# A graph network kernel on one core: dense stage without GpSimd, sort stage with bias matmuls over all rows

## The reference, cut to what matters

```python
# L0, five times: message = h[src] * e * scale, summed by dst
h = leaky(x @ W1[l] + b1[l]) @ W2[l] + b2[l]
e = leaky(edge_attr_32 @ We1[l] + be1[l]) @ We2[l] + be2[l]
# L1: sum of neighbours, with degrees
rst = segment_sum((x * deg_out ** -0.5 @ weight)[src], dst) * deg_in ** -0.5 + bias
# L2, twice: attention over the edges, softmax over the edges of each dst, 2 heads
# L3: relu(x[src] + edge_attr_64), summed by dst
```

## Time and profile before

| what | us |
|---|---|
| median of 3 runs (8425.77 to 8462.65) | 8448.33 |
| the profiled execution, its own time | 8526.05 |
| its span, first to last instruction | 8524.4 |
| TensorE busy | 6618.3 (78%) |
| VectorE busy | 6072.1 (71%) |
| GpSimd busy | 3765.3 (44%) |
| ScalarE busy | 3076.6 (36%) |

### The profile page before, as it was taken

The page is one execution under the profiler, slowest core; times in us unless marked ns, Lnnn a source line. Parts: engine busy times, 40 slices in busy tenths (PEclk is TensorE's granted clock), DMA queues, the critical chain, the costliest instruction groups (busy, mean ns, idle before and its releaser), DMA issues. The chain is left out here.

```text
span 8524.4 us, 285239 instructions
## 1 busy us (share of the span) xinstructions
PE 6618.3 (78%) x79417; PEld 5068.7 (59%) x79424; DVE 6072.1 (71%) x17993; ACT 3076.6 (36%) x5080; POOL 3765.3 (44%) x5536
## 2 busy tenths in 40 slices
PE   5999999934444588788788787887777999999787
PEld 3555655623333467576566666665675777677676
DVE  7444444479999798789788798898554554455799
ACT  2443434412222444344343343343222333233344
POOL 2655666644443255355354454454994000000354
PEclk9888888865555798789798898888555999899999
DMA  3655555622222677577576576675232111111476
GB/s 85 168 163 158 164 163 164 168 54 56 57 57 56 193 174 176 129 176 175 131 175 165 139 175 151 154 175 145 104 116 84 67 64 44 60 69 63 109 191 168
DMA packets 1739057, 1083.39 MB, mean 127 GB/s; under 512 B 1256693, under 2 KB 1623980, under 8 KB 1729274
## 3 DMA queue, kind: packets, MB, share of 16 engines
q1 hardware_dynamic: 1105530, 739.41, 29.9%
q0 software_dynamic: 254336, 267.05, 13.7%
q10 hardware_dynamic: 379008, 74.48, 4.9%
HBM read 812.49 MB, written 266.72 MB: 127 GB/s over the span
## 5 line engine op out<-in xcount | busy, mean ns | idle before, releaser
L540 POOL DMA_DIRECT2D big<-rows x3384 | 1819.6, 538 | 3258.7 <-issue 2189.2
L1307 PE MATMUL ps<-big 128*128 128x64 bf16 x27072 | 1722.9, 204 | 528.8 <-DVE big L1753 312.8
L1307 PEld LDWEIGHTS ps<-big 128*128 128x128 bf16 x27072 | 1330.2, 102 | 890.4 <-issue 624.6
L810 POOL DMA_INDIRECT rows<-big x800 | 1007.6, 1260 | 754.3 <-ACT big L938 409.0
L1295 PE MATMUL ps<-big 128*128 128x64 bf16 x27072 | 1098.2, 202 | 102.2 <-DVE big L1768 41.3
L1295 PEld LDWEIGHTS ps<-big 128*128 128x128 fp8e4 x27072 | 988.6, 104 | 202.0 <-issue 145.5
L1034 ACT CAST big<-big 128x512 bf16<-128x512 f32 x940 | 581.2, 618 | 1153.5 <-DVE big L1781 1153.5
L1559 DVE SCALAR_TENSOR_TENSOR big<-big 128x1000 f32<-128x1000 f32 (+1 forms) x300 | 359.1, 1197 | 860.0 <-ACT big L923 603.5
L1040 ACT CAST big<-big 128x512 bf16<-128x512 f32 x1128 | 697.2, 618 | 586.6 <-issue 436.2
L1781 DVE TENSOR_TENSOR big<-ps,big 128x512 f32<-128x512 f32 x940 | 645.8, 687 | 275.2 <-PE ps L1295 261.8
L1256 PE MATMUL ps<-identb,big 128*128 128x128 bf16 x1504 | 341.4, 301 | 563.1 <-DVE big L1669 561.5
(11 more groups left out here) (259 smaller groups left out, 10337.1 us busy)
## 6 DMA issues: line engine op xcount, KB each, us to landing
big<-ohsD SPq DMA_DIRECT2D x564, 256.0 KB, 2.9
big<-ohdD SPq DMA_DIRECT2D x564, 256.0 KB, 3.5
big<-rows POOLq DMA_DIRECT2D x3384, 32.0 KB, 2.8
big<-rows SPq DMA_DIRECT2D x3384, 32.0 KB, 2.4
big<-maskD SPq DMA_DIRECT2D x50, 1600.0 KB, 6.6
big<-rows ACTq DMA_DIRECT2D x2256, 32.0 KB, 2.5
big<-keyT SPq DMA_DIRECT2D x100, 488.3 KB
maskD<-big SPq DMA_DIRECT2D x25, 1600.0 KB, 6.1
```

The costliest lines, as they stand in the source:

```text
L540: eng.dma_start(edge[:, s.r, j, :], rows[bass.ds(v[s.r * (hi - lo) + j - lo], P), col]).then_inc(landed[s.r], 16)
L810: pool.indirect_dma_start(out=rows[:, :], out_offset=bass.IndirectOffsetOnAxis(ap=sidx[0:EP, j, c:c + 1], axis=0), in_=stage[0:EP, j, c, : ...
L1307: last = pe.matmul(pacc[:, bass.ds(w[j], D)], hot[:, g.r, j * P:(j + 1) * P], parts[:, g.r, c, j * D:(j + 1) * D], start=False, stop=False ...
```

## The change

In the dense stage GpSimd has no work. `find_over` goes to ScalarE as a ReLU of c - 65534 (1 at saturation, 0 otherwise), and the product with `excess` goes into VectorE's addition. ScalarE takes the logarithm of 2 c + tiny instead of c + tiny, and the mask is min(1e28 * log, log) in one VectorE instruction: the logarithm of a count of 0 is negative and becomes about -4e29, those of counts above 0 are positive and stay. `far` and its semaphore are gone. ScalarE copies the even groups of each block and VectorE the odd ones (before: by the running number). In the sort stage the bias matmul takes all 128 rows, with zeros in `be2p` below the third, and the matmuls of zeros are 12 ahead of m = 0 in chunks with j = 0 alone and 1 ahead of each other bias matmul.

```diff
 GpSimd
-            def find_over(w, c):
-                pool.wait_ge(craw_loaded[w % RAW], 16 * (w // RAW + 1))
-                if w >= 2:
-                    pool.wait_ge(cfull_made, (w - 2) * CUTS + c + 1)
-                span = slice(c * CW, (c + 1) * CW)
-                pool.tensor_scalar(over_full[w % 2][:, span], craw[w % RAW][:, span], FULL, excess[:, 0:1], ALU.is_ge, ALU.mult).then_inc(over_made, 1)
-
-            def make_far(w, c):
...
-                pool.tensor_scalar(far[w % 2][:, span], cfull[w % 2][:, span], -1.0, -FAR, ALU.add, ALU.mult).then_inc(far_made, 1)
...
 ScalarE
+            def find_over(w, c):
+                act.wait_ge(craw_loaded[w % RAW], 16 * (w // RAW + 1))
+                if w >= 2:
+                    act.wait_ge(cfull_made, (w - 2) * CUTS + c + 1)
+                span = slice(c * CW, (c + 1) * CW)
+                act.activation(over_full[w % 2][:, span], craw[w % RAW][:, span], ACT.Relu, bias=step2[:, 2:3]).then_inc(over_made, 1)
...
-                act.activation(lnc[w % 2][:, span], cfull[w % 2][:, span], ACT.Ln, bias=tiny[:, 0:1]).then_inc(ln_made, 1)
+                act.activation(lnc[w % 2][:, span], cfull[w % 2][:, span], ACT.Ln, scale=2.0, bias=tiny[:, 0:1]).then_inc(ln_made, 1)
...
-                if tau % 2:
+                if k % 2 == 0:
...
+            for k in range(2 * CUTS):
+                find_over(k // CUTS, k % CUTS)
             for w in range(W):
                 for k in range(TURNS):
                     keep_counts(w, k)
                     if k < CUTS:
                         log_counts(w, k)
+                    elif w + 2 < W:
+                        find_over(w + 2, k - CUTS)
+                if w + 2 < W:
+                    for c in range(TURNS - CUTS, CUTS):
+                        find_over(w + 2, c)
 TensorE, sort
-                    for _ in range(12 if m == 0 else 0):
-                        pe.matmul(bank(4), zerob[:, :], each(iota1b[:, :], 4), start=True, stop=True)
-                    pe.matmul(to, onesb[0:3, 0:EP], be2p[0:3, p, :], start=True, stop=False, skip_group_check=True)
+                    for _ in range(12 if m == j == 0 else 1):
+                        pe.matmul(bank(4 + h), zerob[:, :], each(iota1b[:, :], 4), start=True, stop=True)
+                    pe.matmul(to, onesb[:, 0:EP], be2p[:, p, :], start=True, stop=False, skip_group_check=True)
 VectorE
+            dve.memset(step2[:, 2:3], 1.0 - FULL)
+            bc(dve.memset(be2p[:, :, :], 0.0))
...
-                    dve.wait_ge(far_made, (w - 1) * CUTS)
-                dve.tensor_tensor(cfull[w % 2][:, span], over_full[w % 2][:, span], craw[w % RAW][:, span], ALU.add).then_inc(cfull_made, 1)
+                dve.scalar_tensor_tensor(cfull[w % 2][:, span], over_full[w % 2][:, span], excess[:, 0:1], craw[w % RAW][:, span], ALU.mult, ALU.add).then_inc(cfull_made, 1)
...
-                if tau % 2 == 0:
+                if k % 2:
...
-                dve.wait_ge(far_made, w * CUTS + c + 1)
-                dve.tensor_tensor(lnc[w % 2][:, span], lnc[w % 2][:, span], far[w % 2][:, span], ALU.min).then_inc(mask_done, 1)
+                dve.scalar_tensor_tensor(lnc[w % 2][:, span], lnc[w % 2][:, span], STEEP, lnc[w % 2][:, span], ALU.mult, ALU.min).then_inc(mask_done, 1)
```

More of the change, by code:

```diff
@@ L48 @@
 FULL = 65535.0
+STEEP = 1e28
 JB = 4
@@ L135, in graph_kernel @@
         rowb = sb("rowb", [P, 3, D])
-        step2 = sb("step2", [P, 2])
+        step2 = sb("step2", [P, 3])
         tiny = sb("tiny", [P, 1])
@@ L287, in graph_kernel @@
         lnc = [carve(NP) for _ in range(2)]
-        far = [carve(NP) for _ in range(2)]
         ct = carve(CTS, 512)
@@ L408, in graph_kernel @@
         ln_made = sem("ln_made")
-        far_made = sem("far_made")
         mask_done = sem("mask_done")
@@ L1369, in _, with kept @@
                 last.then_inc(n_down, 1)
+            EVEN, ODD = (TURNS + 1) // 2, TURNS // 2
+            def kept(tau):
+                w, k = tau // TURNS, tau % TURNS
+                if k % 2:
+                    pe.wait_ge(ct_kept_v, w * ODD + k // 2 + 1)
+                else:
+                    pe.wait_ge(ct_kept_a, w * EVEN + k // 2 + 1)
             def turn_counts(w, k):
@@ L1375, in turn_counts @@
                 if tau >= 4:
-                    pe.wait_ge((ct_kept_v, ct_kept_a)[tau % 2], tau // 2 - 1)
+                    kept(tau - 4)
                 for a, v in enumerate(range(4 * k, min(4 * k + 4, W))):
@@ L1382, in sum_rows @@
                 tau = w * TURNS + k
-                pe.wait_ge((ct_kept_v, ct_kept_a)[tau % 2], tau // 2 + 1)
+                kept(tau)
                 if k == 0 and w >= 2:
```

## The result

The changed kernel takes 8220.69 us (median of 4 runs, 8166.69 to 8294.69) beside 8440.91 us (4 runs, 8425.77 to 8462.65) for the kernel before: a ratio of 0.9716, with a 95% interval of 0.9662 to 0.977. The run of 8294.69 us counts as slow and is left out of the ratio, which compares the means of the others (8202.69 and 8442.56 us), but not out of the median. By the medians it is faster by 220 us; forecast were 7946 us and a range from 7830 to 8150. The profiled execution took 8223.66 us, with a span of 8221.4.

What follows compares the result with a forecast made beforehand. It took TensorE and its clock to bound the sort stage and GpSimd the dense stage. Savings of 300 us in the sort and 202 us in the dense stage, off the 8448 us median, gave 7946 us, range 7830 to 8150.

Steps and rivals of the forecast that it cites:

- (e) to (j): Dense stage: GpSimd's 20.6 us a block go, its work moving to ScalarE and VectorE; a saving of 202 us.
- (i): Dense stage, order of work: raw counts loaded late by SP could hold ScalarE's copies and TensorE, 0 to 1 us.
- (j): Dense stage: block of 12.5 us, between VectorE's bound and a cold TensorE's, with the clock between 0.6 and 0.9.
- dense stage cold: Rival: TensorE stays at 1.2 GHz in the dense stage, 15.9 us a block, saving 117 us there, 8031 us; chance 0.18.
- ScalarE reloads tables: Rival: two table loads of 1.28 us a block in the dense stage, 11.9 us for ScalarE, some 7970 us; chance 0.03.
- (a): Sort stage, matmuls of zeros: 4.25 fewer a chunk on average, 0.93 us less, hiding nothing but a PSUM copy.
- (b): Sort stage, bias matmul over all rows instead of three: 0.96 us less a chunk, bounds 0 and 1.2.
- (c): Sort stage at 2.4 GHz: TensorE 11.6 us a chunk, GpSimd the floor at 12.4, giving TensorE 0.8 us of slack.
- (d): Sort stage, clock: a fall costs about 3.5 us without the zeros; 0.9 us a chunk after slack, result 13.3 us.
- Sort keeps its falls: Rival: full rows in the bias don't stop the sort's clock falls, 15.0 us a chunk, 8116 us; chance 0.12.
- the pair of both rivals: Dense stage stays at 1.2 GHz and the sort's clock falls continue, both together: 8201 us; chance 0.03.
- Slower, the sort's clock never comes back: Rival: in the three sort chunks of four without the 12 zeros; mean 20 us a chunk, 8616 us; chance 0.04.

Runs made afterwards that it cites:

- the repeat: The kernel before, profiled once more with no edit: 8436.91 us.
- the edit of SP's order: SP loads attributes before the landing wait, which moves one chunk later: 0.9518, 0.9476, 0.9513 of before on the changed kernel; 0.9615 with the old sort matmuls.
- even zeros: Changed kernel with 8 matmuls of zeros ahead of m = 0 in every chunk, instead of 12 in one of four: 8160.22 us, ratio 0.9666.
- sort part alone: Kernel before with only the full-row bias and the few matmuls of zeros, dense stage unchanged: 8420.66 us, ratio 0.9989.
- changed, new order (third chip): Changed kernel with attributes loaded ahead of SP's landing wait, which moves one chunk later, run on the third chip: 8014.56 us, ratio 0.9476.
- few zeros, three rows: Kernel before with only the matmuls of zeros edited as in the change, bias still over three rows: 8698.31 us, ratio 1.02.
- twelve zeros, full rows: Changed kernel with the matmuls of zeros put back to 12 ahead of m = 0 in each chunk: 8268.58 us, ratio 0.9701.

## Why the prediction was wrong

**Dense stage, (e) to (j): right.** 202 us were forecast, 215 measured (8432.72 - 8217.7). The mask took the lower of its two prices (0.98, forecast 1.00), the flags 0.956 (0.96), the addition with a product 1.045 (1.00). (i) had 0 to 1 us a block for late counts; ScalarE waits 20.5 us for them in 25 blocks, 0.8 each, and TensorE 14.4 us in all for ScalarE's copies. (j) took the middle between the bound by VectorE and that by a cold TensorE, and the clock of 0.73 lies between 0.6 and 0.9 as forecast. The rival "dense stage cold" is refuted, and with it what the Trainium skill, "TensorE: Matmul & The Clock Gate", Part 4, would have made of it: that the turns keep the fast clock off this stage. The page speaks of turns alone, and this stage mixes them with products; in this mix 354 of the 625 turns ran wholly at the granted clock of 1.00. TensorE's timeline in the changed dense stage:

```profile
6053.21 1.00 PE L1387 MATMUL ps<-big 128*128 128x64 f32 x8
6054.05 0.60 PE L1378 MATMUL ps<-ident,big 128*128 128x128 f32 x4
6054.49 1.00 PE L1387 MATMUL ps<-big 128*128 128x64 f32 x8
```

Turn group and product take 1.28 us together, exactly what the earlier trace rows show at 2.4 GHz. "ScalarE reloads tables" is refuted by the one load.

**(a), (b) and the sum at full clock in (c): right.** A full-clock chunk was to shrink from 13.5 to 11.6 us on average over the four j, and 13.61 once and 10.92 three times give 11.6. The Trainium skill, "TensorE: Matmul & The Clock Gate", says in its table of advice ("Why this matters for your kernels") that a single matmul over 32 rows takes as long as one over 128. For 3 rows beside 128 the trace disagrees, with 0.36 beside 0.21 us. With what the Trainium skill, same page, Part 2, says of the weight load it agrees: the one of L1209 over 3 rows took 0.13 us, that of L1200 over 128 rows 0.14.

**The 300 us of the sort stage: wrong.** Measured is 8432.72 - 8420.66 = 12 us. Three steps failed: the start of the sum, the slack of (c), and the price of a fall of the clock in (d).

The first is the start of the sum, "16.3 us each". It came from one execution whose sort was slow, by itself or by its chip; the repeat shows 15.36. The last sentence of the sum then took the savings of that execution off the median of others. The execution was 78 us above that median, and the difference to the repeat sits in the stage that the change touched. Of the 3.0 us a chunk that were forecast, 1.0 were not there in the repeat. The other 1.8 are the 13.3 us that were forecast beside 15.1 measured.

The second is step (c), "the staging ring of four chunks evens out the heavier j = 0", and with it "TensorE gets 0.8 us of slack". The prediction never priced SP's queue: SP loads the keys after waiting for landed scatters. A faster TensorE reaches the keys before they have come, stops for up to 7.5 us, loses the clock and then delivers ids late, for which GpSimd waits; GpSimd's late scatters are what SP waits for next. The slack was not free time at full speed but a stop. That this closes into a loop is read from the order in the code and one timeline. Shown are key waits from 62 to 176 us with the sort edit alone, the timeline at 909 us, and the edit of SP's order, which leaves the sort matmuls as they are: it takes away most of the waits for keys (VectorE's are 135 us in the changed kernel, 28 and 22 in two of the three with the order), and with it the same sort edit is worth 89 us instead of 12. Not shown: which of the two loads that this edit moves does it, and why the stop falls on chunks with j = 0, with even zeros too.

The third is (d): a fall of the clock without the 12 zeros was priced at 3.5 us, less the slack, and "what would show it" asked for a clock over 0.9; it is 0.84. Beyond the 11.6 us at full clock a chunk takes 15.1 - 11.6 = 3.5 us, where the sum had 0.8 of slack and 0.9 for falls, 1.7 together. The number of falls isn't what was off: 54 in 99 chunks are the forecast's "every second". The traces hold the clock's changes, so they can be counted against the stops. A stop here is an idle of TensorE of over 1 us ahead of the look-up matmuls; a fall is a change of the granted clock from 1.00 to 0.50 in the sort's chunks; it stands behind a stop if it came within 8 us of the stop's start.

| kernel | stops | of them with a fall | falls | us at 1.2 GHz, behind stops | other us at 1.2 GHz |
|---|---|---|---|---|---|
| before, first profile | 4 | 4 | 62 | 38 | 420 |
| before, repeat | 20 | 19 | 37 | 195 | 96 |
| sort part alone, same chip | 49 | 39 | 45 | 416 | 27 |
| changed | 39 | 36 | 54 | 382 | 79 |
| changed, new order (third chip) | 20 | 14 | 41 | 133 | 143 |
| few zeros, three rows | 0 | 0 | 81 | 0 | 1126 |
| twelve zeros, full rows | 14 | 13 | 83 | 113 | 382 |

On one chip, with one profile each, the sort edit brought the low time that stands behind no stop from 96 us down to 27, which is what (d) hoped for, and the low time behind stops from 195 up to 416. In the changed kernel 461 us in 54 falls are 8.5 us at half the clock for each, which is an estimated 4.3 us of lost time at most, and the stops come on top. The table also shows that there are two ways to lose the clock. In the first profile of before, and in the two kernels in the last rows, 58 of 62, 81 of 81 and 70 of 83 falls stand behind no stop for keys. What brings those about is open.

**The rivals.** "Sort keeps its falls" was the nearest: it named the clock that stays where it was (0.84 to 0.86), at a mean of 15.0 us (measured 15.14). It came out 105 us below the result because it was subtracted from the slow execution's 16.3 as well. By its number the pair of both rivals, 8201 us, was nearest, but by luck: its half on the dense stage is refuted. "Slower, the sort's clock never comes back" did not happen here, but is a real mechanism: with few zeros and a three-row bias the clock is 0.68. What spoke against it, that the down-projections behind the low stretch are now wholly full-row, was right: that is the one thing in which this run differs from the sort part alone, at 0.85. The full rows hold the clock at 0.84, not above 0.9.

## What to carry to other kernels

Before pricing what a faster engine brings, write down what each of its inputs waits for, through the queues that only issue transfers as well: a load that stands behind a landing wait in an in-order queue can come late once its consumer speeds up, and here 36 of 39 such stops, most of them of 2 us or more, were followed by a fall of TensorE's clock. Where the clock comes and goes, take the chunk time from more than one execution and more than one chip, and take a saving from the execution that it was worked out in.

The best version found is the change with SP's attributes loaded early, 0.9476 to 0.9518 of before in three sets of runs, and its next bound is GpSimd's 12.8 us a chunk.

## What was not expected of the hardware

- What the matmuls of zeros are worth depends on their neighbours. Under the three-row bias the clock of the sort is 0.86 to 0.90 with 12 zeros a chunk and 0.68 with few; under the full-row bias it is 0.84 to 0.85 either way (the runs are on different chips).
- The second of the two loads of features and attributes, that of the attributes, holds SP for 5.1 us (median of 100 in the changed kernel, 2.4 to 9.7); SP's other issues in the timeline shown take 0.3 to 0.4.
- With a drain behind each memset on GpSimd and indirect DMAs ahead, the second memset starts 3.4 us after the end of the first in the chunk shown (median 3.5 over 100 chunks).
- The kernel before has medians from 8433 to 8534 us on the chips used, so only ratios on one chip can be compared.
